# A Mamba block and a mixture of experts on one core: the last two state products on VectorE, and six early results sent between the later ones

## The reference, cut to what matters

```
h   = exp(dt * A) * h + (dt * u) * B        # for each of 16 states, along the tokens
y   = sum over states of h * C;  y = (y + u * D) * silu(z);  x = layernorm(x + y @ W_out)
top two experts of x @ w_g for each token, softmax over the two
rank of a token in its expert's list, kept while rank < 640 (all first choices count before the second ones)
out = sum over both choices of weight * (gelu(x @ c_fc[e]) @ c_proj[e]);  x = layernorm(x + out)
```

## Time and profile before

| | |
|---|---|
| median of three runs | 379.1 |
| the three runs | 375.52, 379.1, 379.96 |
| the profiled execution, whole | 374.95 |
| its span, first to last instruction | 373.0 |
| mean granted TensorE clock | 0.928 of full speed |
| busy: PE, DVE, POOL, ACT | 288.9, 288.7, 263.5, 220.3 |
| moved by DMA | 43.42 MB, mean 116 GB/s |

### The profile page before, as it was taken

The page is one execution under the profiler, slowest core; times in us unless marked ns, Lnnn a source line. Parts: engine busy times, 40 slices in busy tenths (PEclk is TensorE's granted clock), DMA queues, the critical chain, the costliest instruction groups (busy, mean ns, idle before and its releaser), DMA issues. The chain is left out here.

```text
span 373.0 us, 5866 instructions
## 1 busy us (share of the span) xinstructions
PE 288.9 (77%) x1784; PEld 220.9 (59%) x1784; DVE 288.7 (77%) x479; ACT 220.3 (59%) x450; POOL 263.5 (71%) x227
## 2 busy tenths in 40 slices
PE   7797899787877757965764799788579799999700
PEld 6445456654765434755653474344579799999700
DVE  2699889999999799999889799998777233333755
ACT  2858988969966595877776756680422233333305
POOL 3707589977988799978989986898474655455612
PEclk9999999899999977999788699899999999999965
DMA  7161079545253453541222247100316322002773
GB/s 202 43 228 58 2 228 259 190 163 167 86 158 117 127 158 104 189 121 57 83 88 71 78 150 237 31 8 29 81 57 170 109 67 63 27 28 88 206 213 114
DMA packets 36847, 43.42 MB, mean 116 GB/s; under 512 B 3958, under 2 KB 27387, under 8 KB 36816
## 3 DMA queue, kind: packets, MB, share of 16 engines
q1 hardware_dynamic: 33392, 37.85, 33.5%
q0 software_dynamic: 2304, 4.24, 3.4%
q10 hardware_dynamic: 1120, 0.97, 0.9%
HBM read 30.64 MB, written 12.79 MB: 116 GB/s over the span
## 5 line engine op out<-in xcount | busy, mean ns | idle before, releaser
L1515 POOL TENSOR_TENSOR product<-state,c_wide 128x1024 f32<-128x1024 f32 x64 | 149.8, 2345 | 37.8 <-DVE state L1765 24.6
L1138 ACT ACTIVATE psum<-dt,a_neg 128x512 f32<-128x512 f32 x86 | 57.6, 684 | 33.2 <-DVE state L1765 31.8
L730 PE MATMUL psum<-ident,product 128*128 128x128 f32 x384 | 56.7, 297 | 15.9 <-POOL product L1515 15.8
L730 PEld LDWEIGHTS psum<-ident,product 128*128 128x128 f32 x384 | 48.0, 153 | 26.6 <-POOL product L1515 23.0
L1765 DVE TENSOR_TENSOR_SCAN state<-psum,drive 128x512 f32<-128x512 f32 x50 | 59.7, 1213 | 3.8 <-ACT psum L1138 3.6
L1414 ACT ACTIVATE u<-psum 128x512 f32<-128x512 f32 x40 | 23.8, 597 | 59.1 <-PE psum L1006 43.1
L1736 DVE TENSOR_TENSOR drive<-dtu,psum 128x1024 f32<-128x1024 f32 x45 | 54.0, 1200 | 4.4 <-PE psum L697 4.3
L1765 DVE TENSOR_TENSOR_SCAN state<-psum,carry,drive 128x512 f32<-128x512 f32 x40 | 50.4, 1270 | 0.2
L1598 POOL DMA_INDIRECT slot_rows<-sent,scatter_at x32 | 33.8, 1057 | 11.0 <-issue 6.7
L1650 POOL DMA_INDIRECT result_rows<-state,result_at x24 | 23.5, 978 | 20.6 <-DVE state L2037 16.8
L2037 DVE TENSOR_SCALAR state<-psum,tags 128x128 f32<-128x128 f32 x32 | 11.2, 351 | 33.6 <-PE psum L1018 32.5
(11 more groups left out here) (302 smaller groups left out, 612.7 us busy)
## 6 DMA issues: line engine op xcount, KB each, us to landing
c_wide<-c_rows SPq DMA_DIRECT2D x32, 512.0 KB, 4.5
slot_rows<-blank SPq DMA_DIRECT2D x8, 325.0 KB, 4.7
c_wide<-slot_rows SPq DMA_DIRECT2D x8, 325.0 KB
result_rows<-zeros SPq DMA_DIRECT2D x8, 256.0 KB, 5.1
late_rows<-zeros SPq DMA_DIRECT2D x8, 256.0 KB
c_wide<-result_rows SPq DMA_DIRECT2D x8, 256.0 KB
x_tok<-in_x SPq DMA_DIRECT2D x4, 256.0 KB, 6.8
c_wide<-late_rows SPq DMA_DIRECT2D x4, 256.0 KB, 3.8
```

Source lines behind the costliest of these rows:

```text
L730: last = nc.tensor.matmul(y_part(j, d), product[:, i, d, j * P:(j + 1) * P], ident[:, :], is_transpose=True, start=False, stop=True, skip_ ...
L1138: nc.scalar.activation(psum[:, A_BANK + d, :], dt[:, q % 2, d, :], ACT.Exp, scale=a_neg[:, n:n + 1]).then_inc(decay_ready, 1)
L1515: nc.gpsimd.tensor_tensor(product[:, U % PRODUCTS, channels, :], state[:, U % RING, channels, :], wide, ALU.mult).then_inc(product_ready, 1)
```

## The change

VectorE makes the whole product of state 62, between the scans of 62 and 63, and both halves of state 63; GpSimd's last product is that of state 61. TensorE's waits for them become waits for `last_product_ready`. `count_early` moves behind `gate_last`. The early rows' home in `c_wide` moves to the slots that are free first, and SyncE's early loads wait for product 59 rather than for the last ones. The first two experts' second weights are centred by ScalarE, before the last quarter's squares, and have a semaphore of their own. TensorE warms up with 8 instead of 16 products; all four `turn_early` and `copy_early` stand at the head; `turn_rows(0)` stands behind `second_product(6)`, and `first_product(8)` behind `second_product(7)`. GpSimd sends two early results first and then one behind each of the first six experts' late results. Three semaphores of constants become one.

```diff
@@ home of the early rows
+        EARLY_HOME_READ = LAST - C_SLOTS * C_PAIR + 1 + -(-N_EXP * ROW // CH)
-        rows_in = rows_all[:, 0:ROW_SETS * SLOT_TILES * ROW]...
-        early_rows = rows_all[:, ROW_SETS * SLOT_TILES * ROW:(ROW_SETS * SLOT_TILES + N_EXP) * ROW]...
+        early_rows = rows_all[:, 0:N_EXP * ROW]...
+        rows_in = rows_all[:, N_EXP * ROW:(N_EXP + ROW_SETS * SLOT_TILES) * ROW]...
@@ SyncE
-            sp.wait_ge(product_ready, LAST + 1)
-            sp.wait_ge(last_product_ready, 1)
+            sp.wait_ge(product_ready, EARLY_HOME_READ)
             for e in range(N_EXP):
                 sp.dma_start(early_rows[:, e, :], slot_rows[bass.ds(starts[e], P), :]).then_inc(early_loaded[e // 2], 16)
             sp.wait_ge(seconds_sent, 16 * TILES)
             sp.wait_ge(firsts_sent, 16 * TILES)
+            sp.wait_ge(last_product_ready, 3)
@@ TensorE
-            warm(16)
+            warm(8)
+            turn_early(0)
+            turn_early(1)
             pe.wait_ge(x1_ready, TILES)
             pe.wait_ge(ranks_taken, NQ)
-            pe.wait_ge(weights_loaded, 16 * 2 * N_EXP)
-            turn_early(0)
+            pe.wait_ge(first_weights_loaded, 16 * 4)
+            pe.wait_ge(weights_loaded, 16 * 2 * (N_EXP - 2))
             first_product(0)
+            turn_early(2)
+            turn_early(3)
             for k in range(FFN_TILES):
-                if k + 1 < FFN_TILES:
+                if k + 1 < FFN_TILES and k != N_EXP - 1:
                     first_product(k + 1)
-                if k in (0, 2, 4):
-                    turn_early(1 + k // 2)
+                second_product(k)
                 if k == N_EXP - 2:
                     turn_rows(0)
-                second_product(k)
                 if k == N_EXP - 1:
+                    first_product(k + 1)
                     turn_rows(1)
@@ ScalarE, before square(NQ - 1)
+            def center_proj(e):
+                second = weights_of(e)[1]
+                act.wait_ge(first_weights_loaded, 16 * 4)
+                for h in range(HT):
+                    nc.scalar.activation(squares[:, h, :], second[:, h, :], ACT.Copy, scale=-1.0 / D_MODEL,
+                                         accum_out=proj_sums[:, e, h:h + 1]).then_inc(act_step, 1)
+                first = step.up(HT) - HT
+                for h in range(HT):
+                    act.wait_ge(act_step, first + h + 1)
+                    ins = nc.scalar.activation(second[:, h, :], second[:, h, :], ACT.Identity, bias=proj_sums[:, e, h:h + 1])
+                    ins.then_inc(proj_centered if h == HT - 1 else act_step, 1)
+                step.up(HT - 1)
+            center_proj(0)
+            center_proj(1)
@@ GpSimd
-                multiply(U)
+                if U < LAST - 1:
+                    multiply(U)
...
-            for e in range(N_EXP):
+            for e in range(2):
                 send_early(e)
             for e in range(N_EXP):
...
+                if e < N_EXP - 2:
+                    send_early(2 + e)
@@ VectorE
+            def multiply(U, channels):
+                dve.wait_ge(c_loaded[U // C_PAIR % C_SLOTS], 16 * (U // C_PAIR // C_SLOTS + 1))
+                dve.wait_ge(scanned, DT * (U + 1))
+                dve.wait_ge(summed, DT * (U - PRODUCTS + 1))
+                wide = c_wide[:, U % (C_SLOTS * C_PAIR), :].unsqueeze(1).to_broadcast([P, channels.stop - channels.start, CH])
+                nc.vector.tensor_tensor(product[:, U % PRODUCTS, channels, :], state[:, U % RING, channels, :], wide, ALU.mult
+                                        ).then_inc(last_product_ready, 1)
...
                 scan(U, 1)
+                if U == LAST - 1:
+                    multiply(U, slice(0, DT))
...
-            nc.vector.tensor_tensor(product[:, U % PRODUCTS, d, :], ...)
-            count_early()
+            multiply(LAST, slice(1, DT))
+            multiply(LAST, slice(0, 1))
             gate_last(1)
             gate_last(0)
+            count_early()
             sort(NQ - 1)
...
-            center_proj(0)
-            copy_early(0)
-            center_proj(1)
-            copy_early(1)
+            for g in range(PAIRS):
+                copy_early(g)
+            center_proj(2)
+            tag_early()
+            center_proj(3)
             for e in range(N_EXP):
-                if e + 2 < N_EXP:
-                    center_proj(e + 2)
-                if e in (2, 4):
-                    copy_early(1 + e // 2)
-                if e == 4:
-                    tag_early()
                 if e == N_EXP - 2:
                     mask_rows(0)
+                if e == N_EXP - 1:
                     copy_turned(0)
-                if e == N_EXP - 1:
                     mask_rows(1)
                 take_early(e)
+                if e + 4 < N_EXP:
+                    center_proj(e + 4)
```

More of the change, by code:

```diff
@@ L367, in layer_program @@
         seconds_sent = sem("seconds_sent")
-        minus_half_made = sem("minus_half_made")
+        tail_consts_made = sem("tail_consts_made")
         late_out_ready = sem("late_out_ready")
@@ L382, in layer_program @@
         proj_centered = sem("proj_centered")
+        first_weights_loaded = sem("first_weights_loaded")
         weights_loaded = sem("weights_loaded")
@@ L402, in layer_program @@
         results_loaded = [[sem(f"results{k}_loaded{g}") for g in range(NQ)] for k in range(TOP_K)]
-        sent_tagged = sem("sent_tagged")
         rstd2_ready = sem("rstd2_ready")
@@ L472, in load_weights @@
                 first, second = weights_of(e)
-                sp.dma_start(first, c_fc[bass.ds(e, 1), :, :].rearrange("e p m -> p (e m)")).then_inc(weights_loaded, 16)
-                sp.dma_start(second, c_proj[bass.ds(e, 1), :, :].rearrange("e (h p) m -> p (e h) m", p=P)).then_inc(weights_loaded, 16)
+                loaded = first_weights_loaded if e < 2 else weights_loaded
+                sp.dma_start(first, c_fc[bass.ds(e, 1), :, :].rearrange("e p m -> p (e m)")).then_inc(loaded, 16)
+                sp.dma_start(second, c_proj[bass.ds(e, 1), :, :].rearrange("e (h p) m -> p (e h) m", p=P)).then_inc(loaded, 16)
             def load_rows(e):
@@ L720, in add_to_y @@
                 q = U // D_STATE
-                pe.wait_ge(product_ready, U + 1)
+                if U < LAST - 1:
+                    pe.wait_ge(product_ready, U + 1)
+                else:
+                    pe.wait_ge(last_product_ready, 1)
                 i = U % PRODUCTS
@@ L737, in add_last @@
                 for d in (1, 0):
[L738 to L741, removed]
+                    pe.wait_ge(last_product_ready, 2 if d else 3)
                     nc.tensor.matmul(psum[:, Y_BANK + d, :], ident[:, :], product[:, i, d, :],
@@ L1509, in multiply @@
                 gp.wait_ge(c_loaded[i % C_SLOTS], 16 * (i // C_SLOTS + 1))
-                channels = slice(0, DT if U < LAST else DT - 1)
-                gp.wait_ge(scanned, DT * U + channels.stop)
+                gp.wait_ge(scanned, DT * (U + 1))
                 if U >= PRODUCTS:
                     gp.wait_ge(summed, DT * (U - PRODUCTS + 1))
-                wide = c_wide[:, U % (C_SLOTS * C_PAIR), :].unsqueeze(1).to_broadcast([P, channels.stop, CH])
-                nc.gpsimd.tensor_tensor(product[:, U % PRODUCTS, channels, :], state[:, U % RING, channels, :], wide, ALU.mult).then_inc(product_ready, 1)
+                wide = c_wide[:, U % (C_SLOTS * C_PAIR), :].unsqueeze(1).to_broadcast([P, DT, CH])
+                nc.gpsimd.tensor_tensor(product[:, U % PRODUCTS, :, :], state[:, U % RING, :, :], wide, ALU.mult).then_inc(product_ready, 1)
             def split_bc(q):
@@ L1626, in _ @@
                         gp.wait_ge(rows_cleared, 16 * 2 * CLEARS)
-                        gp.wait_ge(sent_tagged, 1)
+                        gp.wait_ge(tail_consts_made, 3)
                     if n >= PLACE[q] and U < LAST - 1:
@@ L1656, in _ @@
                                               oob_is_err=False).then_inc(late_sent[i], 16)
-            gp.wait_ge(minus_half_made, 2)
+                if e < N_EXP - 2:
+                    send_early(2 + e)
+            gp.wait_ge(tail_consts_made, 3)
             for g in range(POWERS):
@@ L1901, in count_early @@
                 dve.wait_ge(early_counted, 1)
-                dve.wait_ge(minus_half_made, 2)
+                dve.wait_ge(tail_consts_made, 3)
                 firsts, seconds = (psum[:, B_BANK + 1, k * N_EXP:(k + 1) * N_EXP] for k in range(TOP_K))
@@ L1935, in _ @@
                         place_weights(q - 1)
-            U, d = LAST, DT - 1
-            dve.wait_ge(c_loaded[U // C_PAIR % C_SLOTS], 16 * (U // C_PAIR // C_SLOTS + 1))
-            dve.wait_ge(scanned, DT * (U + 1))
-            dve.wait_ge(summed, DT * (U - PRODUCTS + 1))
-            nc.vector.tensor_tensor(product[:, U % PRODUCTS, d, :], state[:, U % RING, d, :], c_wide[:, U % (C_SLOTS * C_PAIR), :],
-                                    ALU.mult).then_inc(last_product_ready, 1)
```

(8 more changed lines are left out.)

10 lines of the change are left out of this document (5 added, 5 removed).

## The result

The changed kernel took 379.78 us in the median of 20 runs (377.49 to 382.4), the kernel before 378.0 in 20 runs measured beside it (373.32 to 381.95): ratio 1.0093, 95% interval 1.0067 to 1.0119. Of 378.0 that is 3.5 us slower, inside 2% but clearly not nothing, and on the other side of the forecast of 2.0 faster. The ratio leaves out runs more than 1.5% above the fastest of their kernel, seven of the 20 before and none of the 20 after; with all runs the medians lie 1.8 apart, so that the size of the loss is less sure than its sign. The profiled execution took 377.49, with a span of 375.8, against 374.95 and 373.0; it is the fastest of its 20.

The account below looks back on a forecast made before the run. TensorE's unbroken products from 294.79 us, some 57 us, and what follows were taken as the bound. Starting them 2.6 earlier and adding 0.6 behind them gave -2.0: 379.1 to 377.1 us, range 371.5 to 381.5.

Parts of the forecast that it names:

- Products, count, early loads: Scans' end and early rows: `project_last_x` at 254.7, `project_last` 1.4 later, `early_from` at 260.7, first early load 0.3 later.
- routing runs later: Last quarter: routing 1.5 or 1.6 later, shifting SyncE's first full load from 280.30 to 281.4 to 281.8.
- Six results one by one: Early results sent among late tiles: five sends, 6.5 against TensorE's 7.7, no queue; 0 to 1.3 added after products, 0.6 taken.
- The order of the early tiles: Early tiles before the late ones: transposes and copies first, products then at 0.89 each, ending at 284.8 with VectorE keeping up.
- so the early tiles no longer hold it back: First late tile: late rows decide its start, 286.9 instead of 287.39, 0.5 earlier.
- after it: First late tile to unbroken stretch: 4.1 needed plus idle time; stretch 1.4 to 3.8 earlier, middle 2.6 taken.
- Clock, the rival at 0.18: Waits before `project_last_x` and after the warm-up halve TensorE's clock, 1.7 lost each, together 3.4: 380.5; chance 0.18.
- The stops rival at 0.2: Idle time behind the first late tile stays and the result loads cost all: -1.4 + 1.3 = -0.1, 379.0; chance 0.2.

Follow-up runs that it names:

- calm series: First three follow-up series: kernel before took 370.46, 370.25 and 370.19; no gelu in their twelve traces starts more than 0.4 behind its product's end.
- the fifth series: Changed kernel with 16 warm-ups and all early sends first, old against new order of early tiles: 1.0022 and 1.0013 against the kernel before, which took 377.66 or 376.9.
- series with stops: Last two follow-up series: kernel before took 376.9 and 377.66; longest gelu delay behind a product's end is 3.2 to 6.2 in these and the first measurement's traces.

## Why the prediction was wrong

*Products, count, early loads*: right in their places within 0.7. That routing runs later was over-priced (0.55 measured, 1.5 forecast), and with it the first full load.

Two steps failed, each by 2 to 3 us.

*Six results one by one: "no queue builds up", 0.6.* The sum over an expert was right, five sends of 1.27 in 7.7. But I had averaged over the expert. The extra send stands directly between two others, so three stand in a row, and where stops come ScalarE and VectorE are held up beside each such run. Putting the sends first takes 2.8 to 3.9 us off the time there, and 3.0 to 3.6 off the late tiles; in the first measurement the late tiles lost 2.57. In calm series the step costs 0.6 us in the median (the kernel before with it), and no cost at all is inside its interval, so that its agreement with my 0.6 says little; the mean time behind TensorE's end is 20.97 in the ten traces with spread sends and 20.63 in the ten without.

*"The order of the early tiles", "so the early tiles no longer hold it back", and with it the 2.6 of "after it".* The early tiles were to be over at 284.8, and the late rows were to decide, at 286.9. In all 14 traces with the new order, calm or not, the first late tile starts as the last early tile's second product ends, and in 13 of them TensorE never waits for the late rows. So what the early tiles lose is paid in full. In the first measurement they ended at 290.83: 2.61 idle in a stop, and the rest mostly at the half clock, where the first product took 1.92 instead of 1.06 and the three groups behind the stop 1.40, 1.91 and 1.69. What comes behind the first late tile went better than forecast (4.22, where I had put about 5.3), and both together made 0.15 of loss. I took the middle between no stops and all stops, 2.4 us of them, for the place where they had been. What I had not seen is that the stops come beside GpSimd's runs of scatters, and that all eight scatters of the last quarter run beside the early tiles. There the new order puts the first gelus and results into that run with only the first tiles' products made, and TensorE waits: 2.6 to 4.5 in the six traces with stops. That the new order makes the stops there longer is seen in all six against the two with the old order; its price in time was tried in the fifth series alone, where the centrings move with the order, and can't be told from nothing.

*Clock, the rival at 0.18*: it came, though not at `project_last_x`. In the first measurement's trace the clock was 0.50 from 264.7 to 271.5, behind 2.41 without work ahead of the short warm-up, and again behind the stop. By the timed edit on the kernel before, 8 for 16 costs 1.7 us in a calm series. That it equals the price of one fall that I had worked out is luck in part: the trace of that edit has one stretch three times as long. With stops it can't be seen. The Trainium skill ("TensorE: Matmul & The Clock Gate", What's actually happening) has activity release the throttle; the timed edit agrees with it, by these 1.7. But the traces with 16 or 24 warm-up products have such falls too, seven of twelve, against six of eight with 8.

*The stops rival at 0.2* had the right mechanism and a price that stopped at -0.1, since I let them come back only where they had been.

What an edit has shown of the loss is the spread sends: some 3 us in a series with stops, timed there and not in the first measurement. Without them the changed kernel is no slower there than the kernel before (0.9969, 0.9928 to 1.001). That the clock and the stops in the early tiles took the order's gain is read from the traces and was not timed by an edit of its own under stops. In calm series the same kernel is within 0.4% of the one before, 1.0033 and 0.9996. The version with 16 warm-ups and the sends first was run in three series: 0.9968, 0.998 and 1.0013. Only the first excludes no change.

Open: what a stop is. The traces show it beside runs of sends, in the slower series only, and the same eight scatters in a row in calm series without any. The kernel is the same in both kinds, so what differs between the series isn't in the program; no run shows what it is. That longer spacing of the scatters would take the early stops away wasn't tried.

## What to carry to other kernels

When two paths meet, work out both with their losses before one is called free: here the path that "no longer holds" was the one that held. Price an instruction that is put into a queue by the longest run that it makes, not by the queue's mean load over a loop. Take a stall that no row explains as something that can move to wherever the change puts work, and give it both ends, larger than seen as well. Before a difference of 1% is read as a property of a kernel, run it in more than one series: here the kernel before itself moved by 2%.

## Unexpected of the hardware

- One kernel took 370.46 us in one series and 377.66 in another, both on chip 0 by the record, with starts of ScalarE and VectorE up to 6 us behind products that had ended in TensorE's records, only in the second.
- In the eight traces with stops these lie in runs of two to eight indirect scatters of GpSimd, some 0.30 apart, or within 3 us behind one, and there is none in stretches where the scatters stand singly.
- The clock fell to 0.50 for 3.4 or 6.8 us between 260 and 285 us in traces with 8 and 16 warm-up products and for 3.4 with 24, and for 10.2 us in the kernel before with 8.
